# One pass per layer norm tile: 192 features written once, the second block transposed as 64 columns

## The reference, cut to what matters

```
h = patches(x) @ W_proj + b_proj ;  class token in front
h = h + attention(layernorm(h))     # 4 expert branches, 12 heads of 16, causal window of 64,
                                    # fused, gated: silu(f @ w_gate.T) * (f @ w_up.T)
h = h + ffn(layernorm(h))           # per token one of 4 experts (argmax), 192 -> 768 gelu -> 192
layernorm(x) = (x - mean) / sqrt(var + 1e-5)     # over the 192 features
```

## Time and profile before

| | |
|---|---|
| median of 3 runs | 4546.69 us (4549.31, 4537.58, 4546.69) |
| the profiled execution: span, first to last instruction | 4535.8 us; what lies around it is not listed for it, the median is 10.9 us above the span |
| PE busy | 3887.5 us, 86% |
| DVE busy | 3545.3 us, 78% |
| ACT busy | 3031.1 us, 67% |
| POOL busy | 1091.8 us, 24% |
| the loop | about 91 us to 4084 us of the span |
| the expert stage | about 4108 us to the end |

### The profile page before, as it was taken

The page is one execution under the profiler, slowest core; times in us unless marked ns, Lnnn a source line. Parts: engine busy times, 40 slices in busy tenths (PEclk is TensorE's granted clock), DMA queues, the critical chain, the costliest instruction groups (busy, mean ns, idle before and its releaser), DMA issues. The chain is left out here.

```text
span 4535.8 us, 119272 instructions
## 1 busy us (share of the span) xinstructions
PE 3887.5 (86%) x41326; PEld 2848.8 (63%) x41326; DVE 3545.3 (78%) x9897; ACT 3031.1 (67%) x9620; POOL 1091.8 (24%) x1496
## 2 busy tenths in 40 slices
PE   3888888888888888888888888988888888886998
PEld 2666666666666666666666666666666666664776
DVE  4888878887888888788878888887788778885665
ACT  2777767776677777667766777776677667772433
POOL 0222222222222222222222222222222222221222
PEclk7999999999999999999999999999999999997999
DMA  5122221111111222221111111222111111125664
GB/s 180 40 51 51 51 50 47 46 46 47 38 37 47 51 51 51 51 49 47 47 45 46 29 48 48 51 51 51 48 47 46 45 45 30 47 51 179 220 219 163
DMA packets 254292, 292.98 MB, mean 65 GB/s; under 512 B 69289, under 2 KB 236755, under 8 KB 244098
## 3 DMA queue, kind: packets, MB, share of 16 engines
q1 hardware_dynamic: 230242, 214.47, 18.4%
q10 hardware_dynamic: 4608, 38.73, 2.8%
q0 software_dynamic: 18912, 32.58, 2.1%
HBM read 127.06 MB, written 43.10 MB: 38 GB/s over the span
## 5 line engine op out<-in xcount | busy, mean ns | idle before, releaser
L865 ACT ACTIVATE p_s<-bank,smin 128x128 f32<-128x128 f32 (+1 forms) x6144 | 1821.6, 375 | 183.5 <-DVE smin L946 163.6
L946 DVE TENSOR_REDUCE smin<-bank 128x3 f32<-128x384 f32 (+1 forms) x2048 | 1135.7, 555 | 218.3 <-PE bank L722 189.8
L742 PE MATMUL bank<-ident_s,p_s 128*128 128x128 f32 (+1 forms) x6144 | 885.2, 253 | 28.4 <-DVE pt_f L951 7.9
L717 PE MATMUL bank<-masks_s,mask_id_s 128*128 128x384 f16 (+1 forms) x2048 | 675.7, 330 | 30.7 <-DVE qt_f L917 16.4
L742 PEld LDWEIGHTS bank<-ident_s,p_s 128*128 128x128 f32 (+1 forms) x6144 | 602.1, 142 | 139.2 <-issue 103.9
L722 PE MATMUL bank<-stacks_f 128*128 128x256 f16 (+3 forms) x4096 | 680.1, 247 | 0.0
L892 POOL TENSOR_TENSOR w_s<-o_raw 128x192 f32<-128x192 f32 (+1 forms) x512 | 306.9, 600 | 1184.2 <-DVE o_raw L939 1184.2
L951 DVE TENSOR_TENSOR pt_f<-bank,pt_f 128x384 f16<-128x384 f32 x1024 | 553.3, 540 | 0.0
L248 PE MATMUL bank<-zt,wqkv_s 128*128 128x394 f16 x1920 | 395.7, 369 | 171.1 <-PEq L1009 161.6
L856 ACT CAST pt_f<-bank 128x384 f16<-128x384 f32 x1024 | 510.8, 499 | 0.0
L722 PEld LDWEIGHTS bank<-stacks_f 128*128 128x128 f16 (+1 forms) x4096 | 431.6, 105 | 123.0
(11 more groups left out here) (130 smaller groups left out, 6358.9 us busy)
## 6 DMA issues: line engine op xcount, KB each, us to landing
stacks_f<-qt_f SPq DMA_DIRECT2D x768, 73.9 KB, 2.1
stacks_f<-kt_f SPq DMA_DIRECT2D x1536, 36.9 KB, 2.1
wx_t<-wx_d SPq DMA_DIRECT2D x36, 1344.0 KB
x_raw<-x_t_dram ACTq DMA_DIRECT2D x32, 1182.0 KB
rec_t<-rec_d SPq DMA_DIRECT2D x36, 678.0 KB, 4.2
rec_d<-fill_s SPq DMA_DIRECT2D x5, 678.0 KB, 4.1
stacks_f<-w_dram SPq DMA_DIRECT2D x2, 1536.0 KB
wx_d<-w_s SPq DMA_DIRECT2D x8, 384.0 KB
```

The costliest lines, as they stand in the source:

```text
L717: nc.tensor.matmul(ps, mask_id_s[:, 0:rows], masks_s[:, m0:m0 + HU * kn], start=True, stop=False)
L742: mm = nc.tensor.transpose(turned[:, j * rows:j * rows + rows], p_slot(u)[:, k0:k0 + 128], ident_s[0:rows, 0:rows])
L865: ins = nc.scalar.activation(p_slot(s)[:, j * kn:j * kn + kn], bank[s % SR][0:rows, j * kn:j * kn + kn], ACT.Exp, scale=-1.0, bias=smin[0: ...
L946: nc.vector.tensor_reduce(least, ps, AX_X, ALU.min).then_inc(S["min_ready"], 1)
```

## The change

`z` has 192 columns in place of 256, and `rec` (features, z2, token number) has 388 in place of 452. `normalise` issues one instruction for each tile. The second transpose takes 64 columns and fills 64 partitions of its bank. `high_of` and `zt_high` write only partitions 0 to 63 of the second block; `low_of` and `zt_low` read bank and high half in partitions 0 to 63 and write the difference to partitions 64 to 127. What `zt[:, 2]` holds is as before.

```diff
+Z_BLOCKS = ((0, 128), (128, D - 128))
-IDC = D + 256
+IDC = D + D
-        z = sb1("z", [128, 4, 256])
+        z = sb1("z", [128, 4, D])
...
                 for blk in range(2):
-                    mm = nc.tensor.transpose(bank[b0 + blk][:, c0:c0 + rows],
-                                             z[0:rows, tt, 128 * blk:128 * blk + 128], ident_s[0:rows, 0:rows])
+                    f0, fn = Z_BLOCKS[blk]
+                    mm = nc.tensor.transpose(bank[b0 + blk][0:fn, c0:c0 + rows], z[0:rows, tt, f0:f0 + fn],
+                                             ident_s[0:rows, 0:rows])
...
-            for blk in range(2):
-                nc.scalar.copy(target[:, 2 * blk, 0:TP], bank[b0 + blk][:, 0:TP]).then_inc(S[his], 1)
+            for blk, (_, fn) in enumerate(Z_BLOCKS):
+                nc.scalar.copy(target[0:fn, 2 * blk, 0:TP], bank[b0 + blk][0:fn, 0:TP]).then_inc(S[his], 1)
...
-            nc.vector.tensor_tensor(target[64:128, 2, 0:TP], bank[b0 + 1][64:128, 0:TP], target[64:128, 2, 0:TP],
+            nc.vector.tensor_tensor(target[64:128, 2, 0:TP], bank[b0 + 1][0:64, 0:TP], target[0:64, 2, 0:TP],
                                     ALU.subtract).then_inc(S[los], 1)
...
-            for z0, z_n, s0 in ((0, D, 0), (D, 64, 128)):
-                ins = nc.vector.tensor_scalar(z[0:rows, tt, z0:z0 + z_n], src[0:rows, tt, s0:s0 + z_n],
-                                              mv[0:rows, tt, 0:1], rstd[0:rows, tt:tt + 1], ALU.subtract,
-                                              ALU.mult)
-            ins.then_inc(S[ready], 1)
+            nc.vector.tensor_scalar(z[0:rows, tt], src[0:rows, tt], mv[0:rows, tt, 0:1], rstd[0:rows, tt:tt + 1],
+                                    ALU.subtract, ALU.mult).then_inc(S[ready], 1)
```

More of the change, by code:

```diff
@@ L1147, in turn_tile @@
                         for k in range(TK):
-                            c0 = D + 128 * blk
-                            mm = nc.tensor.transpose(bank[Z_BANK + blk][:, 128 * k:128 * k + 128],
-                                                     rec_t[:, j % RS, k, c0:c0 + 128], ident_s[:])
+                            f0, fn = Z_BLOCKS[blk]
+                            mm = nc.tensor.transpose(bank[Z_BANK + blk][0:fn, 128 * k:128 * k + 128],
+                                                     rec_t[:, j % RS, k, D + f0:D + f0 + fn], ident_s[:])
                     mm.then_inc(T["zt_mm"], 1)
@@ L1191, in zt_high @@
                         act.wait_ge(T["hid_mm"], HM * (j - ZS + 1))
-                    for blk in range(2):
-                        nc.scalar.copy(zt_t[:, j % ZS, 2 * blk, :], bank[Z_BANK + blk][:, 0:TS]
+                    for blk, (_, fn) in enumerate(Z_BLOCKS):
+                        nc.scalar.copy(zt_t[0:fn, j % ZS, 2 * blk, :], bank[Z_BANK + blk][0:fn, 0:TS]
                                        ).then_inc(T["zt_hi"], 1)
@@ L1227, in zt_low @@
                     dve.wait_ge(T["zt_hi"], 2 * j + 2)
-                    nc.vector.tensor_tensor(zt_t[64:128, j % ZS, 2, :], bank[Z_BANK + 1][64:128, 0:TS],
-                                            zt_t[64:128, j % ZS, 2, :], ALU.subtract).then_inc(T["zt_lo"], 1)
+                    nc.vector.tensor_tensor(zt_t[64:128, j % ZS, 2, :], bank[Z_BANK + 1][0:64, 0:TS],
+                                            zt_t[0:64, j % ZS, 2, :], ALU.subtract).then_inc(T["zt_lo"], 1)
                 def finish(j):
```

## The result

The changed kernel takes 4500.23 us (median of 4 runs, 4497.74 to 4500.71) against 4548.0 us before (4 runs, 4537.58 to 4551.56). The ratio is 0.9901, with a 95% interval of 0.9887 to 0.9916: 1.0% faster, some 45 us. The forecast was 4528; the measured time is close to that of rival A, 4501.5, at the lower edge of the range.

What follows compares the result with a forecast made beforehand. PE bounds the expert stage; in the loop its waits and clock falls matter. Saving 1.38 us an iteration, less 0.82 of added falls, times 32, and 1 us once, gave -18.9 us: 4528 us, range 4500 to 4553.

Steps and rivals of the forecast that it cites:

- rival A: Whole loop: all the direct saving arrives, falls keep today's mean of 1.61 us; -45.2 us, 4501.5 us; chance 0.15.
- What bounds the kernel: PE without a gap in the expert stage; in the loop PE's waits at both norms and 1.80 us ahead of the logits.
- the falls of the clock: In loop iterations PE's clock drops for a while from 2.4 to 1.2 GHz; each costs 1.62 us, today 52 us altogether.
- DVE, per norm, 0.89 us: Both norms: four 64-column `normalise` instructions go, the eight's 2.05 us becomes 1.16, saving 0.89 us.
- Second norm: Second norm: PE's last transpose and everything to the end of the projections come 0.89 us earlier.
- First norm: First norm: POOL's `rstd` is next, so only 0.49 us is saved; PE's wait falls from 0.97 to 0.48.
- quiet iteration: Loop iteration in which the clock keeps full speed: 123.28 us before, forecast 1.38 shorter at 121.90.
- PE and copies at 0, DMA small: Second transposes and second-block copies: 0; DMA records 14% shorter, fill on the path once, -0.5 us.
- rival D: Norms' low halves: DVE reading partitions 0 to 63 and writing 64 to 127 could be slower, costing 38 us; chance 0.03.
- The clock takes part of it back: Loop: clock drops rise from 1.61 to 2.43 us an iteration, +0.82, with one in half the iterations and two in half.
- near or under 1.61: Loop: the prediction's sign of being wrong, if clock drops average near or under 1.61 us an iteration.
- The base: Whole kernel: before's profiled span 4535.8 us, shown median 10.9 us above it, so the forecast starts from 4546.7.

Runs made afterwards that it cites:

- the second norm alone: Only the second norm and its shorter records changed, against the kernel before; first norm as before: 4528.0 us, ratio 0.9964.
- 123.28 to 122.79 alone: Only the first norm (z) written once and transposed as 64 columns, against the kernel before; second norm and records as before: 4519.37 us, ratio 0.9947.
- the wide kernel: Against the kernel before, only duplicate DVE instructions dropped and low halves read from partitions 0 to 63; z, records, second transpose and copies stay wide: 4506.21 us.
- the changed kernel with 400 idle columns: Changed kernel plus a DVE memset over 400 columns at each iteration's end, where PE waits for the barrier: 4521.9 us.
- the kernel before with 0.4 us of padding: Kernel before plus a DVE memset over 400 columns at each iteration's end: 4534.7 us, ratio 0.9981.
- the four kernels that lack it: Changed kernel with z2 copied ahead of images (4469.09 us); also with first norm's tiles 2, 3 behind low half (4470.89), plus 200 (4470.36) or 400 (4471.67) idle columns.
- three kernels: The changed kernel (4500.23 us), and the kernel before with only its first norm changed (4519.37 us) or only its second (4528.0 us).
- where the order of work was changed: Changed kernel with first norm's tiles 2 and 3 behind the low half (4470.62 us), or with ScalarE copying z2 ahead of the images (4469.09 us).
- A loop can settle on one length: Changed kernel with first norm's tiles 2, 3 behind the low half and z2 copied ahead of images: 4470.89 us; with 400 idle columns 4471.67.

## Why the prediction was wrong, point by point

**What bounds the kernel**: right. PE's waits at the two norms and the pause ahead of the logits were the places, and the expert stage stayed at 10.86 us a tile. That the falls of the clock decide a large part of the time was right too. One reading was off and changed nothing: the z2 transposes of before end 8.92 us after the first matmul and not 8.7, and now at 8.02, so the 0.9 us between them is as forecast.

**DVE, per norm, 0.89 us**: right. Second norm 0.89 (123.28 to 122.39 alone). First norm 0.49: measured 0.49 (123.28 to 122.79 alone), PE's wait 0.47 where 0.48 was forecast, DVE's wait for POOL 0.30 where some 0.4 was. The quiet iteration of the changed kernel is 1.37 us shorter, where 1.38 was forecast.

The Trainium skill's figure (VectorE: DVE Perf Modes, TRN2 errata) would have made the four instructions worth 0.38 us by the prediction's estimate; the run with the second norm alone shows 0.89. The same section says itself that this row is too low for the duration of a single operation. The measurement decides.

**PE and copies at 0, DMA small**: right in the loop; the wide kernel has the same four lengths. A DVE operation that reads partitions 0 to 63 and writes 64 to 127 is not slow (560 to 563 ns for L293, where the one of before, L291, took 571 on average), so rival D is out.

**The clock takes part of it back**: this step failed. "Half of the iterations with one fall, half with two", 2.43 us, measured 1.76. The difference, 0.67 x 32 = 21.4 us, is the whole of the miss span to span: 39.9 us gained where 18.9 were forecast. The forecast's 1.5 falls an iteration were 46 in 31; the traces have 31 before and 30 after. By its own sign, "near or under 1.61", the prediction was wrong here. The direction of the argument was not absurd: the second norm alone has 2.21 and the changed kernel with 400 idle columns 2.18. But I had no row that gave a size, and took the middle between the value of before and the worst. Nothing showed that a value above it is likelier than one below: the kernel before with 0.4 us of padding has 1.09. That the changed kernel came out near the value of before, and not at the 2.2 of its neighbours, is luck as far as these runs show. Within what the 1.76 is made of, one part was not foreseen at all: now that PE hardly waits for the second norm, a slow stretch at the start that reaches far costs PE time. With up to 8.04 us for the first 30 matmuls, against 6.48 in iteration 0, the transposes end up to 0.70 us late, 0.26 on average. Before, the first 30 took up to 7.53 us, and the wait for DVE covered it: the transposes ended at 8.93 us at the latest in every iteration.

**The base**: the falls of before were read in its profiled execution, the fastest of its four. The median of 4548.0 lies 10.4 us over it, so if all that is falls, typical ones were near 1.61 + 10.4 / 32 = 1.93 us; the 17 runs of before in a later set (4543.8) give 1.80, and the same sum for the changed kernel, 2.5 us over its profiled execution, 1.84. Against that the falls hardly changed, and rival A's sum, -45.2 us, agrees with the ratio. Its chance of 0.15 was too small: with no evidence for a direction, "as today" was the middle case.

The Trainium skill's rule (TensorE: Matmul & The Clock Gate, "HAM oscillation") that pauses bring the half clock back is borne out: without the pause of 1.8 us no fall follows at that place, in any iteration of the four kernels that lack it. It gives no size for a loop like this.

## What to carry to other kernels

Where iterations of equal work differ in length by a fixed amount, split the time into the quiet length and the rest. The direct saving of removed instructions was forecast to 0.02 us on the quiet length in three kernels; where the order of work was changed, the forecasts were off by 0.2 and 1.0 us. The rest can move by as much as a change saves, either way, and with no evidence for a direction its middle estimate is the mean of before. A single comparison of two kernels in such a loop does not tell what an edit is worth; an idle instruction that changes the length shows how much is luck. And falls that are removed at one place can come back at another, so count them at both. Look at the engine that hands over a small statistic (POOL's `rstd`), and put work that another engine waits for ahead of the instruction that waits for it.

## What the runs showed of the hardware that was not expected

- Adding idle time made a kernel faster: 0.45 us an iteration, ratio 0.9981 (0.9971 to 0.9990), with 21 falls to 1.2 GHz behind the logits and in `gate_up` in 31 iterations in place of 31.
- A loop can settle on one length (122.83 to 122.94 us, 31 times), and 0.4 us of padding then costs nothing (4470.9 and 4471.7 us).
- A VectorE operation over 16 columns took 2.22 us on average in place of 0.42 when another order of the copies let it start further ahead of the end of POOL's 4.7 us subtraction, and 0.18 with no subtraction beside it. In the changed kernel, too, it runs beside that subtraction in 31 of 33 cases, started nearer to its end. That POOL's operation is the cause is inferred from the common end of the two, in 128 cases of four kernels; it was not tried apart.
- A 64-column instruction of `normalise` held DVE for 0.22 us and one of three times as many columns for 0.29.
